# A decoder layer on one core: key reads, one weight load and the causal tile move in their queues

## The reference, cut to what matters

```python
q = (x @ Wq).reshape(b, t, 32, 32).transpose(0, 2, 1, 3)
k = (x @ Wk).reshape(b, t, 8, 32).transpose(0, 2, 1, 3)
v = (x @ Wv).reshape(b, t, 8, 32).transpose(0, 2, 1, 3)
q, k = _apply_rope(q, cos, sin), _apply_rope(k, cos, sin)
scores = jnp.einsum('bhqd,bhkd->bhqk', q, repeat(k, 4)) / math.sqrt(32)
scores = jnp.where(causal, jnp.finfo(scores.dtype).min, scores)
ctx = softmax(scores) @ repeat(v, 4)
x = x + ctx @ Wo
```

## Time and profile before

| | |
|---|---|
| median of 3 runs | 481.53 us (477.95 to 482.09) |
| profiled execution, its own time | 480.98 us |
| its span, first to last instruction | 479.1 us |
| granted clock of TensorE, mean | 0.993 |
| PE busy | 441.4 us, 92% |
| DVE busy | 377.3 us, 79% |
| ACT busy | 300.1 us, 63% |
| POOL busy | 288.1 us, 60% |

### The profile page before, as it was taken

One profiled execution on the slowest core, in us unless ns is written; L12 is line 12 of the kernel. 1 busy time (PEld: TensorE's weight loads), 2 busy tenths in 40 slices (PEclk: granted clock), 3 DMA queues, 4 the chain that ended last, 5 costly groups with the idle time before them and its releaser, 6 DMA issues.

```text
span 479.1 us, 9721 instructions
## 1 busy us (share of the span) xinstructions
PE 441.4 (92%) x3730; PEld 243.4 (51%) x3730; DVE 377.3 (79%) x961; ACT 300.1 (63%) x302; POOL 288.1 (60%) x157
## 2 busy tenths in 40 slices
PE   0899997998999999999999999998998999899896
PEld 0676453554555555555555555555543444446442
DVE  4989873888788888888978899896297568799775
ACT  3586252123787777787778898889745313797633
POOL 5002463143989999999998888888730980707000
PEclk9999998999899999999999999999999999999999
DMA  8563386612041111101153113333087010000044
GB/s 328 179 248 126 115 269 207 212 45 78 28 152 46 47 57 57 55 27 46 48 174 118 45 75 111 114 112 108 25 284 266 23 45 23 1 1 2 2 177 179
DMA packets 21042, 50.93 MB, mean 106 GB/s; under 512 B 4736, under 2 KB 10112, under 8 KB 19712
## 3 DMA queue, kind: packets, MB, share of 16 engines
q1 hardware_dynamic: 19696, 41.79, 25.5%
q10 hardware_dynamic: 1296, 8.45, 5.0%
HBM read 40.67 MB, written 9.44 MB: 105 GB/s over the span
## 4 chain that ended last, share of the span: by engine, by line
PE 54%; DVE 14%; ACT 11%; POOL 11%; issue 5%; DMA 4%; SPq 0%; ACTq 0%; DVEq 0%; POOLq 0%
PE ps L1465 11%; PE ps L1288 9%; PE ps L1371 7%; PE ps L1616 5%; ACT s1reg L566 5%; PE ps L1352 5%; POOL more L1205 4%; PE ps L1333 4%; PE ps L1313 4%; DVE stat L769 3%; POOL s1reg L1205 2%; PE ps L1571 2%; DMA qstack<-in_x 2%; PE ps L1354 2%; DMA rope_scratch<-s1reg 2%
## 5 line engine op out<-in xcount | busy, mean ns | idle before, releaser
L829 DVE CUSTOM_DVE_ANT_0 ps<-ps,causal 128x512 f32<-128x512 f32 (+3 forms) x256 | 120.9, 510 | 19.7 <-PE ps L1333 16.6
L566 ACT ACTIVATE s1reg<-ps 128x1280 f32<-128x1280 f32 x64 | 78.9, 1233 | 44.4 <-PE ps L1354 44.1
L1288 PE MATMUL ps<-xT,wqx 128*128 128x512 f16 x384 | 96.3, 383 | 0.0
L1465 PE MATMUL ps<-wo_reg,xT 128*128 128x512 f16 x384 | 93.0, 379 | 0.0
L1333 PE MATMUL ps<-kreg,qstack 96*128 96x512 f16 (+3 forms) x256 | 61.4, 305 | 5.3 <-DMA qstack<-rope_scratch 3.3
L1352 PE MATMUL ps<-qstack,kreg 98*128 98x512 f16 (+3 forms) x256 | 57.9, 303 | 0.0
L1288 PEld LDWEIGHTS ps<-xT,wqx 128*128 128x128 f16 x384 | 37.2, 98 | 37.3 <-issue 2.1
L1465 PEld LDWEIGHTS ps<-wo_reg,xT 128*128 128x128 f16 x384 | 36.5, 97 | 36.6 <-issue 0.2
L1186 POOL TENSOR_TENSOR s1reg<-s1reg 128x512 f32<-128x512 f32 x11 | 15.9, 1449 | 64.0 <-DVE s1reg L818 63.9
L1205 POOL TENSOR_TENSOR s1reg<-s1reg 128x1280 f16<-128x1280 f32 x19 | 49.8, 2623 | 5.9 <-ACT s1reg L572 5.7
L1205 POOL TENSOR_TENSOR wkv<-s1reg,wkv 128x1280 f16<-128x1280 f32 x18 | 47.2, 2624 | 5.5 <-ACT wkv L572 5.5
(11 more groups left out here) (134 smaller groups left out, 929.4 us busy)
## 6 DMA issues: line engine op xcount, KB each, us to landing
s1reg<-in_weights ACTq DMA_DIRECT2D x8, 1024.0 KB, 5.2
s1reg<-in_ctx SPq DMA_DIRECT2D x16, 512.0 KB, 4.2
qstack<-rope_scratch SPq DMA_DIRECT2D x48, 128.0 KB, 2.6
rope_scratch<-s1reg SPq DMA_DIRECT2D x40, 128.0 KB, 2.2
qstack<-in_x SPq DMA_DIRECT2D x8, 512.0 KB, 5.1
s1reg<-in_x SPq DMA_DIRECT2D x16, 256.0 KB, 3.2
out<-s1reg SPq DMA_DIRECT2D x7, 512.0 KB, 2.7
s1reg<-in_L_ffn_weight SPq DMA_DIRECT2D x5, 512.0 KB, 6.1
```

Source lines behind the costliest of these rows:

```text
L566: nc.scalar.activation(ebuf[:, j % 2, :], st_ps[:, 0:SCORES], ACT.Exp, scale=EXP_SCALE, bias=P_LOG_SCALE).then_inc(e_done, 1)
L829: last = nc.vector.tensor_tensor_reduce(part, part, causal[:, T - w:T], 1.0, LOWEST, ALU.add, ALU.max, mt[:, G % 2, h, qt:qt + 1])
L1288: last = mm(out_ap, w(ws, k), xT[:, xs, KT * b + k, :], start=(k == 0 and n == 0), stop=(k == KT - 1 and n == 2))
L1465: last = mm(ps[:, bank, :], xT[:, os, KT * b + k, t], wo_sb[:, ws, 4 * h:4 * h + 4, k, :], start=(k == 0 and n == 0), stop=(k == KT - 1 an ...
```

## The change

Four things move, and nothing is added to the computation.

- In SP's list k_stack(0) goes ahead of to_scratch(2), and k_stack(2) and k_stack(3), the keys of batch 1, go from between the writes of tiles 3 to 4 to behind q_stack(6).
- These two count on a semaphore of their own, keys_b1. The waits of `from_scratch` and of `scores` on stack_ready are lowered by their share, and the scores of group 8, the first of batch 1, wait for keys_b1.
- In ACT's list next_weight(5), the load of chunk 7, goes from behind weight_high(6) to behind rope_high(6); rope_high(6) goes ahead of weight_high(7).
- The causal tile's load goes in SP's list from behind the constant `halves` to behind next_x(7), with a semaphore of its own. DVE waits for it ahead of scores_max(0); DVE's and TensorE's waits on const_in fall from 48 to 32.

```diff
             sp.dma_start(halves[:, :, :], half_t.rearrange("s p t -> p s t")).then_inc(const_in, 16)
-            sp.dma_start(causal[:, :], causal_t).then_inc(const_in, 16)
...
             def from_scratch(n, to, slot, parts):
                 sp.wait_ge(scr_written[n % 2], 32 * (n // 2 + 1))
-                if n >= 2:
-                    sp.wait_ge(stack_ready[n % 2], 48 * (n // 2))
+                if n >= 4:
+                    sp.wait_ge(stack_ready[n % 2], 48 * (n // 2 - 1))
+                ready = keys_b1 if n in (2, 3) else stack_ready[n % 2]
                 for part, hl in enumerate(parts):
-                    sp.dma_start(to[DH * part:DH * part + DH, slot:slot + HG, :], scr[n, :, hl, :, :]).then_inc(stack_ready[n % 2], 16)
+                    sp.dma_start(to[DH * part:DH * part + DH, slot:slot + HG, :], scr[n, :, hl, :, :]).then_inc(ready, 16)
...
             next_x(7)
+            sp.dma_start(causal[:, :], causal_t).then_inc(causal_in, 16)
             to_scratch(0)
             to_scratch(1)
+            k_stack(0)
             to_scratch(2)
-            k_stack(0)
             k_stack(1)
             to_scratch(3)
-            k_stack(2)
             to_scratch(4)
-            k_stack(3)
             q_stack(4)
             to_scratch(5)
             to_scratch(6)
             q_stack(5)
             q_stack(6)
+            k_stack(2)
+            k_stack(3)
             to_scratch(7)
...
             rope_high(4)
             weight_high(6)
-            next_weight(5)
             exp_table()
             v_high(4)
             rope_high(5)
+            rope_high(6)
+            next_weight(5)
             weight_high(7)
-            rope_high(6)
             next_weight(6)
             next_weight(7)
             weight_high(8)
...
-            dve.wait_ge(const_in, 48)
+            dve.wait_ge(const_in, 32)
...
             rotate_b(6)
+            dve.wait_ge(causal_in, 16)
             scores_max(0)
...
                 if n % UNITS == 0:
-                    pe.wait_ge(stack_ready[G % 2], 48 * (G // 2 + 3))
+                    pe.wait_ge(stack_ready[G % 2], 48 * (G // 2 + 2))
+                    if G == KV:
+                        pe.wait_ge(keys_b1, 96)
...
-            pe.wait_ge(const_in, 48)
+            pe.wait_ge(const_in, 32)
```

More of the change, by code:

```diff
@@ L169, in build @@
         ident_in, const_in = sem("ident_in"), sem("const_in")
-        par_in = sem("par_in")
+        par_in, causal_in = sem("par_in"), sem("causal_in")
         xin_in = [sem(f"xin_in{i}") for i in range(4)]
@@ L186, in build @@
         stack_ready = [sem(f"stack_ready{i}") for i in range(2)]
+        keys_b1 = sem("keys_b1")
         s_done, s_max = sem("s_done"), sem("s_max")
```

## The result

The changed kernel took 475.26 us at the median of 6 runs (474.61 to 476.14), the kernel before 481.81 (477.95 to 482.19): ratio 0.9898, 95% interval 0.9856 to 0.994. Twice more, side by side with the kernel before, the ratio was 0.9899 (0.9866 to 0.9931) and 0.9900 (0.9857 to 0.9942). So it is 1.0% faster, some 5 us, by the narrowest of these intervals 3.3 to 6.4 us. The profiled execution took 475.61 us, its span is 473.7.

A forecast was written before the change was run, and what follows sets the result against it. The prediction took TensorE's 3.3 us wait on qstack, and the slow clock after it, as the bound the change removes. 3.3 + 1.5 - 0.7 = 4.1 us off the profiled 480.98 gave 476.9 us, range 475.0 to 480.0.

The forecast's parts named there:

- The hold: Before q_stack(4): tile 4's low-half write took 8.07 us because it lands when chunk 7's load does; without it, 2.2 to 4.1.
- Stall and slow clock: TensorE at scores, near 77 us: removing the 3.3 us wait on qstack and the half-speed clock behind it gains 4.8 us.
- Rotations: DVE's work behind chunks 7 and 8: a 1.4 us wait for chunk 7 fits the slack; chunk 8 takes 6.8 us.
- The loss ahead of q_tile(10, 0): TensorE's wait for rotate_b(8): key reads beside chunk 8 make the tile 0.7 us late.
- The upper end of that term: Chunk 8 beside the key reads: at 8.7 us to land, q_tile(10, 0) loses 2.6 us.
- The second price: Chunk 8 with nine key reads, from a 358 GB/s memory limit: nearer to 8 us, a cost near 2 us.
- (b): Slow clock elsewhere: new dip near 98, 478.4 us, chance 0.10; the one at 121 vanishing, 475.3 us, chance 0.09.
- part 3: Causal tile's load moved behind next_x(7), in the first transfers: cost and gain zero, bounds 0 to +0.6 us.
- the sum: Whole kernel: 3.3 + 1.5 - 0.7 = 4.1 us gained against the profiled 480.98, giving 476.9 us.
- (a): Moved key reads slow chunk 8, or chunk 7 too, to its upper bound: 478.8 to 479.6 us, chance 0.17.
- (d): Both chunks land at 8.7 us, q_tile(10, 0) is 5.9 us late and the clock slows: 483.6 us, chance 0.06.
- (c): The edit doesn't free q_stack(4), whose landing hangs on something other than the load: no change, 481.0 us, chance 0.06.

The follow-up runs named there:

- e1_chunk: Kernel before with only chunk 7's load moved behind rope_high(6), key reads and causal tile left in place; 475.89 us, ratio 0.9918.
- e2_keys: Kernel before with only the key reads reordered and given their own semaphore, chunk 7 and causal tile left in place; 480.18 us, ratio 1.0012.
- e9_table: Kernel before with the key reads reordered and ACT's activation table load moved to behind rope_high(2); 479.96 us, ratio 1.0012.
- e3_causal: Kernel before with only the causal tile's load moved behind next_x(7), with its semaphore and waits; 479.09 us, ratio 0.9989.
- e4_warm: Kernel before with 12 matmuls nobody reads added in the stall ahead of scores(0); 478.23 us, ratio 0.9977.
- a2_full: Changed kernel run again, nothing altered, beside the kernel before; 475.18 us.
- e6_keys_last: Changed kernel with k_stack(2) and k_stack(3) moved further back, behind q_stack(11); 475.22 us.
- e8_half: Changed kernel with chunk 7 in two 512 KB loads, the first at the old place, the second behind rope_high(6); 479.14 us, ratio 0.9992.
- e10_nocausal: Changed kernel with the causal tile's load back at the head of SP's list, timed a second time; 475.98 us.
- a3_full: Changed kernel run once more, nothing altered; 475.40 us.
- e7_nokeys: Changed kernel with the key reads back at their old places; 475.83 us, ratio 0.9908.

## Why the prediction was right, and where it was off

The forecast was 476.9 with 475.0 to 480.0; 475.26 lies inside, near the lower edge, and the way it gave is the one that the runs show.

**The hold.** Right: chunk 7's load holds the write of tile 4. e1_chunk shows it by moving the load alone, and the packets of e2_keys show the write served behind the load. But the text took all of the 8.1 us for the load's. That such a write lands "when the load does" holds for 15 of its 16 shares; the last one landed 1.8 us later in e2_keys and e9_table, behind a packet of instructions. In the kernel before, the chunk's own last share was late too, by 1.8 of its 8.7 us, so that chunk and write landed within 0.4 us of each other and the reading came out. The increment rule of the Trainium skill (DMA: Bandwidth & Descriptors, "Queues, rings and completion order"), cited in the prediction, agrees with the rows of before. It speaks of each DMA engine by itself, so it allows one late share, but those 1.8 us don't come from it.

**Stall and slow clock.** 3.3 + 1.5 = 4.8 us were forecast, 3.34 + 1.57 = 4.91 measured between the profiles. What the text didn't say is that this is one execution of a kernel that spreads over 8 us. In the profile of e2_keys (2.2 us of stall) the clock stayed full, in that of e3_causal (2.6 us) it fell, and e4_warm, with the stall and the full clock, took 478.2 us at the median.

**Rotations.** Chunk 7 issued at 78.4 and landed in 5.3, forecast; 77.2 and 5.4, measured, the same with 1.2 us of earlier start. DVE's wait was forecast as 1.4 us and was 1.51. Chunk 8: 6.8 forecast, 6.4, and 6.8 in a2_full. The loss ahead of q_tile(10, 0) was forecast as 0.7 and was 0.44. e6_keys_last, where chunk 7's wait stayed and the time too, points to that wait and not to the key reads beside chunk 8. The upper end of that term was real: e8_half reached it by a change that looks harmless, 9.3 us and 2.5 us of stall, against 8.7 and 2.6 in the text. The second price, from the Trainium skill's figure for the memory (DMA: Bandwidth & Descriptors, "Where 436 GB/s comes from"), made it a chunk of nearly 8 us, an estimate that was too high for this order. (It took nine reads as 1.15 MB where they are 1.18, and rival (b)'s 475.3 should read 475.4; neither matters.)

**The term that may have failed** is part 3, "Cost and gain zero", with bounds "0 to +0.6". It left no room for a gain, though the load leaves the head of the queue in which the first input tiles are fetched. The two pairs with and without it point to -0.6 and -0.8 us, outside these bounds, but not clear of the noise. And the sum was made against one profile without pricing the luck of its first 74 us: v_tile(5) began at 74.67 there, the latest of all profiled runs with part 3 in its old place (73.47 to 74.15 in the others). Part 3 and this luck together are 1.24 us between the two profiles; how they divide isn't shown. With 0.11 more from stall and clock and 0.26 less lost ahead of q_tile(10, 0), and 0.34 for the lead that shrinks from 5.7 to 5.4 behind it, that makes the 1.27 us by which the gain between the profiled executions, 480.98 - 475.61 = 5.37, exceeds 4.1.

**The rivals.** (a) and (d) did not happen here, but their mechanism did in e8_half. (b) came half true: the slow stretch at 121 vanished, and it gave nothing, since the attention loop had won its loss back. The prediction priced that at 1.5 us; it is 0 by group 2. From the first exponential of group 0 to that of group 2 it is 29.08 us in both profiles, and 29.07 or 29.08 in e4_warm, e8_half and e6_keys_last, which have such a stretch. It isn't always free: with one at 115 to 116 in e1_chunk and e10_nocausal it is 29.27 and 29.34, and with one at 114.2 in a3_full 29.95. (c) is refuted by e1_chunk.

## What to carry to other kernels

When a small transfer on the critical path is slow, look at what else was issued within a few us on the other queue: a large load that nobody needs yet may be holding it; here moving that load gained some 4 us and reordering the small ones alone nothing. Look at the packets as well: a landing is that of the slowest of 16 shares, and one packet of another queue can hold that one back. A transfer that is moved out of one place lands in another: find the next large load whose margin is thinnest, and check how early the moved reads can start, because a faster step ahead of them (e8_half) can push them into it. A stall of TensorE may cost its own length or, as here, half as much again, by luck of the clock, so one that is removed can take spread off the kernel as well as time.

## What the runs showed of the hardware

A write of 128 KB from SP's queue, issued while a 1 MB load ran on ACT's, landed in 3.4 to 8.4 us, against 2.0 to 3.0 mostly with no load about. In e2_keys, e9_table and e8_half none of its packets began before the load's first share was through (72.02, 71.20 and 69.06). A packet of 16 KB of the kind "instruction" took 0.9 to 1.7 us; where the whole of it fell into the write, the last of 16 shares landed 1.6 to 2.1 us behind the others, with a load beside it (e2_keys, e9_table, e8_half) and without (e1_chunk, e7_nokeys, a3_full).

The granted clock fell to 0.50 after TensorE's stall of 3.3 us in the kernel before and after one of 2.6 us in e3_causal, and stayed at 1.00 through one of 2.2 us in e2_keys. The stall near 112 to 119, about 1.7 us in every profile, was followed by a slow stretch in seven of the 14 profiles (before, e1_chunk, e4_warm, e6_keys_last, e8_half, e10_nocausal, a3_full) and by none in the other seven.
